# A four-block conv and attention sequence: second attention on f32r tiles with on-chip layout transfers, and jobs ahead of scores in the first attention

## The reference, cut to what matters

```python
# block 0: neighbourhood attention, 8 heads of 16, window 7x7, gate, layer norm
attn = einsum('bijnd,bijnpqd->bijnpq', q, kn) + bias
out = einsum('bijnpq,bijnpqd->bijnd', softmax(attn), vn) @ proj_w + proj_b
x = layernorm(x + out * sigmoid(relu(x @ g1_w + g1_b) @ g2_w + g2_b))
# block 1: depthwise 3x3 convolution without its centre tap, plus x
x = conv(x, kernel * mask) + x
# block 2: full attention, keys and values from the image padded by 3 (reflect)
energy = einsum('bhdq,bhdk->bhqk', q, k)
out = einsum('bhdk,bhqk->bhdq', v, softmax(energy))
x = gamma * out + x
# block 3: Fourier mixing (AFNO), linear attention, MLP of 8*128, three layer norms
```

## Time and profile before

| what | us |
| --- | --- |
| runs | 628.61, 634.68, 642.61 (median 634.68) |
| profiled execution | 639.11, its span 636.9 |
| PE busy | 548.5 (86%) |
| DVE busy | 387.8 (61%) |
| ACT busy | 356.5 (56%) |
| DMA, mean | 36 GB/s |

### The profile page before, as it was taken

How to read it: one execution, slowest core, us unless ns; L and a number is a source line. 1 busy time by engine, 2 the same in 40 slices (tenths; PEclk the granted TensorE clock), 3 DMA queues, 4 the chain that set the end, 5 groups by cost and what they waited for, 6 DMA issues and landing times.

```text
span 636.9 us, 9303 instructions
## 1 busy us (share of the span) xinstructions
PE 548.5 (86%) x3532; PEld 271.1 (43%) x3532; DVE 387.8 (61%) x719; ACT 356.5 (56%) x705; POOL 38.6 (6%) x47
## 2 busy tenths in 40 slices
PE   5889988998989570899999999999998987677997
PEld 2655664555433300122222223222465474553886
DVE  2546654246646390678888888830645645866986
ACT  1777777457432500267777777788764634405553
POOL 5000000011011200200000000000300000000000
PEclk9999999669898755599999999999998998869999
DMA  8500000000005999000160000000000000000000
GB/s 302 245 2 2 1 3 2 0 1 2 1 0 141 121 175 234 2 2 1 30 72 1 1 2 1 3 1 2 0 1 2 1 1 2 1 0 1 0 34 33
DMA packets 8276, 22.65 MB, mean 36 GB/s; under 512 B 1698, under 2 KB 5026, under 8 KB 7074
## 3 DMA queue, kind: packets, MB, share of 16 engines
q1 hardware_dynamic: 8232, 22.06, 14.9%
HBM read 17.80 MB, written 4.19 MB: 35 GB/s over the span
## 4 chain that ended last, share of the span: by engine, by line
PE 69%; ACT 12%; DVE 6%; DMA 6%; SPq 3%; issue 2%; POOL 0%; ACTq 0%
PE ps L392 62%; PE ps L570 6%; DMA scr<-r_o 3%; SPq L445 3%; ACT r_p L1062 2%; DMA r_stk<-mt 2%; ACT r_p L1054 2%; DVE mx L1426 2%; ACT r_p L1026 1%; ACT r_p L1028 1%; ACT r_p L1165 1%; DVE r_p L1500 1%; DVE r_prt L1494 1%; DMA xt<-in_xT 1%; DVE r_prt L1504 1%
## 5 line engine op out<-in xcount | busy, mean ns | idle before, releaser
L392 PE MATMUL ps<-r_stk 98*128 98x512 bf16 (+3 forms) x768 | 164.1, 418 | 29.0 <-DMA r_stk<-mt 16.0
L1165 ACT ACTIVATE r_p<-ps 128x512 f32<-128x512 f32 x256 | 132.5, 624 | 90.8 <-PE ps L392 90.0
L1426 DVE TENSOR_REDUCE mx<-ps 128x1 f32<-128x1024 f32 x128 | 151.0, 1220 | 50.2 <-PE ps L392 50.1
L392 PEld LDWEIGHTS ps<-r_stk 98*128 98x128 bf16 (+2 forms) x768 | 53.7, 131 | 161.1 <-issue 44.6
L392 PE MATMUL ps<-r_p,r_v 128*32 128x512 f32 (+3 forms) x832 | 81.1, 483 | 0.9 <-ACT r_p L1165 0.9
L1351 DVE CUSTOM_DVE_ANT_0 r_p<-ps,r_tab 128x209 f32<-128x209 f32 (+1 forms) x128 | 45.0, 401 | 35.5 <-PE ps L392 35.5
L1054 ACT ACTIVATE r_p<-r_p,mx 128x209 f32<-128x209 f32 (+1 forms) x128 | 57.8, 483 | 3.5 <-DVE mx L1351 3.4
L1062 ACT ACTIVATE r_p<-ps 95x512 f32<-95x512 f32 (+2 forms) x48 | 28.5, 594 | 41.0 <-PE ps L570 41.0
L570 PE MATMUL ps<-cst,r_p 128*95 128x128 f32 (+2 forms) x320 | 47.3, 290 | 2.0 <-ACT r_p L1054 1.1
L570 PEld LDWEIGHTS ps<-cst,r_p 128*95 128x95 f32 (+2 forms) x320 | 38.5, 158 | 21.3 <-ACT r_p L1054 10.5
L1359 DVE COPY r_p<-ps 95x512 f32<-95x512 f32 (+1 forms) x32 | 22.0, 686 | 27.9 <-PE ps L570 27.9
(11 more groups left out here) (185 smaller groups left out, 676.2 us busy)
## 6 DMA issues: line engine op xcount, KB each, us to landing
r_stk<-scr SPq DMA_DIRECT2D x48, 128.0 KB, 8.2
r_tab<-in_tab SPq DMA_DIRECT2D x4, 836.0 KB, 13.3
r_tab<-in_w SPq DMA_DIRECT2D x1, 2688.0 KB, 16.3
scr<-r_prt SPq DMA_DIRECT2D x4, 384.0 KB, 3.0
scr<-r_o SPq DMA_DIRECT2D x4, 384.0 KB, 17.2
cst<-in_cst SPq DMA_DIRECT2D x1, 1124.5 KB, 17.8
r_tab<-in_tab SPq DMA_DIRECT2D x2, 532.0 KB, 7.6
r_tab<-in_tab SPq DMA_DIRECT2D x1, 1064.0 KB, 9.4
```

The costliest lines, as they stand in the source:

```text
L392: return nc.tensor.matmul(out, lhsT, rhs, start=start, stop=stop, **kw)
L1165: nc.scalar.activation(pa2[:, u % 12, :], ps[:, l2_bank(u), :], ACT.Exp).then_inc(sem("exp2"), 1)
L1426: v.tensor_reduce(mx[:, 4 * h + qt:4 * h + qt + 1], ps[:, bank:bank + 2, :], AXIS.XY, ALU.max)\
```

## The change

- **First attention.** On PE `l0_job(s)` stands ahead of `l0_scores(s+1)`. The head outputs are normalised in place.
- **Between.** Only image 0 is prepared ahead of the second attention: convolution, projections with weights whose columns already stand in the order of the stack (`wq2`, `wk2`: each head three times 16 columns in 64), and the values. Stack 0 is made by ACT (the low part, `lw`) and DVE directly in r_stk as f32r.
- **Stacks.** A part is now f32r: high and low, three products of 16 rows, so a head has 48 rows (with the maximum 50) and two heads share a tile at partitions 0 and 64. Stacks 1 to 3 come from `natural2` projections, which ACT moves to xb and POOL splits into nhi and nlo; SP copies them from SBUF to SBUF, 24 DMAs of 64 KB a stack. POOL blanks the stacks' other rows first (`blank`). The buffer scr and its traffic are gone.
- **Maxima.** A first entry is two products, for two heads, into two banks; DVE takes both maxima over 512 keys at once, 16 entries a unit. `maxima` joins the halves and writes the negated maximum as two f32r columns in zmax; `l2_turn` transposes eight blocks of 128x128 on PE, and DVE adds the result to the stack (entry "max"). No DMA.
- **Order.** `l2_order` writes the firsts, maxima and the other jobs (`L2_JOBS`) in one list; `before` spreads a unit's entries over the first 28 of its 32 second products. The denominators, head sums, norm and convolution of image 1, the projections for stacks 1 to 3 and the values of image 1 stand in it. The list has 31 entries up to the first "max", and then 25, 21, 19, 17, 17, 17 and 15 between one "max" and the next.
- **w3.** SP loads it behind the last exponential, since stack 3 lies in r_tab.

```diff
+L2_JOBS = {(0, 0): ("den", 4, 1), (0, 1): ("den", 5, 1), (0, 2): ("den", 6, 1), (0, 3): ("den", 7, 1), (0, 4): ("nproj", 1, 1), (0, 5): ("nproj", 1, 2),
+           (0, 6): ("heads", 0, 1), (0, 8): ("heads", 0, 2), (0, 9): ("gated", 0, 1), (0, 13): ("centre", 0, 1), (0, 14): ("centre", 0, 2),
+           (1, 0): ("centred", 0, 1), (1, 3): ("variance", 0, 2), (1, 6): ("norm", 0, 1), (1, 8): ("conv", 0, 5),
+           (2, 3): ("nproj", 2, 2), (2, 9): ("nproj", 3, 2), (3, 3): ("values", 1, 2)}
...
+    order = []
+    for n in range(2 * NB):
+        for r in range(16):
+            order.append(("first", n, r))
+            if n and r == 1:
+                order.append(("max", n - 1, 0))
+            if (n, r) in L2_JOBS:
+                kind, i, parts = L2_JOBS[n, r]
+                if n == 0:
+                    order.append((kind, i, parts - 1))
+                else:
+                    order += [(kind, i, k) for k in range(parts)]
+    order.append(("max", 2 * NB - 1, 0))
...
+    for n in range(2 * NB):
+        a = at["max", n, 0] + 1
+        b = at["max", n + 1, 0] + 1 if n + 1 < 2 * NB else a
+        before += [a + min((k + 1) * (b - a) // 28, b - a) for k in range(32)]
+    return order, slot, done, at, before
 W3 = [("wq3", C), ("wk3", C), ("wv3", C), ("wo3", C), ("lkg", C), ("lkb", C), ("aw1", 2048), ("aw2", 512),
...
-            sp.wait_ge(sem("pv0"), nblk[NU])
-            sp.wait_ge(sem("og"), NT)
-            sp.wait_ge(sem("lnout"), NT)
-            sp.dma_start(stk[96:98, :, 1].rearrange("p s h n -> p s (h n)"),
-                         io["mrows"].rearrange("p h n -> p (h n)").unsqueeze(1).to_broadcast([2, 3, HG * TOK]))\
-                .then_inc(sem("in_ones"), 16)
-            for t in range(NT):
-                store_parts(2, t)
-                if t % 2:
-                    image_stored(2, t // 2)
-                    load_stack(2, 2 * (t // 2))
-                    if t == 1:
-                        load_stack(2, 1)
+                        rows = slice(64 * a + HD * head, 64 * a + HD * (head + 1))
+                        for r in range(3):
+                            src = (nlo if r == 2 - a else nhi)[rows, :].bitcast(F32)
+                            dst = stack(b)[64 * e + HD * r:64 * e + HD * (r + 1), a, pr, :]
+                            sp.dma_start(dst.bitcast(F32), src).then_inc(sem(f"stk2_{b}"), 16)
+            sp.wait_ge(sem("exp2"), 32 * NB2)
             sp.dma_start(r_tab[:, 0:W3N], io["w3"]).then_inc(sem("in_w3"), 16)
-            for n in range(NB2):
-                b, qh = n // 2, n % 2
-                sp.wait_ge(sem("p1_taken2"), U2 * (n + 1))
-                for h in range(HG):
-                    sp.dma_start(stk[K1_L2:K1_L2 + 2, b % 3, 0, h, tile(qh)], mt[8 * h:8 * h + 8, :]).then_inc(sem("mrow2"), 16)
-                if n == 2:
-                    sp.wait_ge(sem("pv2"), 2 * NCH)
-                    load_stack(2, 3)
             for t in range(NT):
...
+            def project2(j, bank):
+                pr, a = j // 2, 1 - j % 2
+                o = W2A[("wq2", "wk2")[a]][0] + C * pr
+                for t in range(2):
+                    last = mm(ps[:, bank + t, :], w2[:, o:o + C], x2[:, tile(t)])
+                last.then_inc(sem("pj2"), 1)
+
+            def natural2(b, t, bank):
+                o = W2A["wn2"][0] + C * (b % NG)
...
                 if s + 1 < NU:
                     l0_scores(s + 1)
-                l0_job(s)

             pe.wait_ge(sem("tt0"), HG * NU)
...
+            def l2_first(n, r, bank):
+                b, qh, pr, qt, kh = n // 2, n % 2, r // 8, r // 2 % 4, r % 2
+                if r % 8 == 0:
+                    if b:
+                        pe.wait_ge(sem(f"stk2_{b}"), 24 * 16)
+                    else:
+                        pe.wait_ge(sem("sp2"), 2 * pr + 2)
+                q0 = qh * TILE + 128 * qt
+                for e in range(2):
+                    rows = slice(64 * e, 64 * e + PARTS)
+                    last = mm(ps[:, bank + e, :], stack(b)[rows, 0, pr, q0:q0 + 128], stack(b)[rows, 1, pr, tile(kh)])
+                last.then_inc(sem("s1_2"), 1)
+
...
+            def l2_turn(n, bank):
+                pe.wait_ge(sem("zmax"), n + 1)
+                for pr in range(2):
+                    for qt in range(4):
+                        o = C * (4 * pr + qt)
+                        last = nc.tensor.transpose(ps[:, bank + pr, C * qt:C * (qt + 1)], zmax[:, o:o + C], ident)
+                last.then_inc(sem("s1_2"), 1)
+
...
+                pr, rows = h // 2, slice(64 * (h % 2), 64 * (h % 2) + PARTS + 2)
+                mm(ps[:, l2_bank(u), :], stack(b)[rows, 1, pr, 128 * c:128 * c + 128],
+                   stack(b)[rows, 0, pr, tile(qh)]).then_inc(sem("s2_2"), 1)

...
+            issued = 0
+            while issued <= at["max", 0, 0]:
+                l2_entry(issued)
+                issued += 1
+            for u in range(32 * NB2):
+                while issued < before[u]:
+                    l2_entry(issued)
+                    issued += 1
+                l2_second(u)
+                if u % 4 == 3 and u > 4:
...
-                                         ACT.Copy, scale=cc("mult")[:, c:c + 1]).then_inc(sem("vev2"), 1)
+                pr, a, bank = j // 2, 1 - j % 2, (2, 0, 4, 6)[j]
+                act.wait_ge(sem("pj2"), j + 1)
+                if j > 1:
+                    act.wait_ge(sem("sp2"), j - 1)
+                nc.scalar.activation(lw[j % 2], ps[:, bank:bank + 2, :], ACT.Identity,
+                                     bias=vv(("lbq_", "lbk_")[a] + str(pr)), scale=vv(("ls_q", "ls_k")[a])).then_inc(sem("low2"), 1)
...
+            def maxima(n):
+                m = mx[:, 32 * (n % 2):32 * (n % 2) + 32]
+                z, zr = (a.rearrange("p (g x) -> p g x", x=64) for a in (zmax, zmaxr[:, :]))
+                dve.wait_ge(sem("p1"), taken[at["first", n, 15]])
+                v.tensor_tensor(mm16[:, :], m[:, 0:16], m[:, 16:32], ALU.max).then_inc(sem("m16"), 1)
+                dve.wait_ge(sem("m16"), n + 1)
+                if n:
+                    dve.wait_ge(sem("s1_2"), taken[at["max", n - 1, 0]])
+                else:
+                    dve.wait_ge(sem("zero_max"), 1)
+                v.tensor_scalar(zr[:, :, PARTS], mm16[:, :], -1.0, None, ALU.mult).then_inc(sem("zhi"), 1)
+                dve.wait_ge(sem("zhi"), n + 1)
+                v.scalar_tensor_tensor(zr[:, :, PARTS + 1], mm16[:, :], -1.0, z[:, :, PARTS], ALU.mult, ALU.subtract).then_inc(sem("zmax"), 1)
...
+                    o = 32 * (i % 2) + 16 * (k % 2) + 2 * (k // 2)
+                    v.tensor_reduce(mx[:, o:o + 2], ps[:, bank:bank + 2, :], AXIS.X, ALU.max).then_inc(sem("p1"), 1)
+                    if k == 15:
+                        maxima(i)
+                elif kind == "max":
+                    b, qh = i // 2, i % 2
+                    dve.wait_ge(sem("s1_2"), taken[e])
+                    v.tensor_tensor(stack(b)[:, 0, :, tile(qh)], ps[:, bank:bank + 2, :], stack(b)[:, 0, :, tile(qh)].bitcast(F32), ALU.add).then_inc(sem("p1"), 1)
...
+                elif kind == "centred":
+                    dve.wait_ge(sem("cen"), 4)
+                    v.tensor_copy(t1b.rearrange("p (b n) -> p b n", b=2), ps[:, 4:6, :]).then_inc(sem("cenb"), 2)
+                elif kind == "norm":
...
+                pool.wait_ge(sem("vev2"), img + 1)
+                if img == 0:
+                    pool.wait_ge(sem("vsum2"), 4)
+                dims = values2(img)[:, :, :, 0:HD]
+                g.tensor_tensor(dims, dims, cc("mult").unsqueeze(2).unsqueeze(3).to_broadcast([C, NCH, NH, HD]), ALU.mult).then_inc(sem("vsc"), 1)
...
+            def blank(b):
+                for a in range(2):
+                    for i, rows in enumerate((slice(32, 64), slice(96, 128))):
...
+                        g.memset(stack(b)[rows, a, :, :].bitcast(F32), float(a)).then_inc(sem("blank"), 1)
+
+            def natural(b):
+                pool.wait_ge(sem("xb"), b)
+                pool.wait_ge(sem("blank"), 4 if b == 1 else 12)
+                if b > 1:
+                    pool.wait_ge(sem(f"stk2_{b - 1}"), 24 * 16)
+                g.tensor_copy(nhi[:, :], xb).then_inc(sem("nhi"), 1)
+                pool.wait_ge(sem("nhi"), b)
+                g.tensor_tensor(nlo[:, :], xb, nhi[:, :].bitcast(F32), ALU.subtract).then_inc(sem("nlo"), 1)
+
```

More of the change, by code:

```diff
@@ L730, in _, with tap @@
[L730 to L756 removed]
+            def tap(t, k, bank):
+                i = PE_TAPS[k]
+                r0 = 16 * (t % 2) + i // 3
+                return mm(ps[:, bank, :], kd[:, i, :], pad[:, t // 2, r0:r0 + 16, i % 3:i % 3 + W], start=k == 0, stop=k == conv_end)
@@ new lines, in _, with slot_free @@
+            pe.wait_ge(sem("lnout"), 2)
+            for t in range(2):
+                for k in range(len(PE_TAPS)):
+                    last = tap(t, k, t)
+                last.then_inc(sem("conv"), 1)
+            pe.wait_ge(sem("in_w2"), 16)
```

(61 more changed lines are left out.)

474 lines of the change are left out of this document (227 added, 247 removed).

## The result

| | before | after |
|---|---|---|
| median of the runs | 632.9 us (628.6 to 642.6) | 666.4 us (658.6 to 668.3) |
| ratio to before | | 1.051, 95% interval 1.045 to 1.057 |
| profiled execution | 639.1 us | 667.2 us, span 665.3 |

Some executions ran at a lower granted clock and took longer; the ratios leave them out, medians and ranges do not, and the profile of before is of one of them. The changed kernel is 5% slower. The prediction was 608 us, range 591 to 631: it has the wrong sign. The stages of the kernel after, answering to the earlier trace rows: the first attention, the preparation, the first unit of scores, units 0, 1, 4 and 7 of the second attention. Columns: window, its length, busy time of PE, PEld, DVE, ACT and POOL, granted clock, DMA share, GB/s.

What follows compares the result with a forecast made beforehand. PE was taken to set the steady pace before, DVE after; in the first attention, a PE-ACT loop. 15 - 34.8 - 8.4 + 1.2 = -27.0 against the profiled 639.1 gave 612, in the median's terms 608 us, range 591 to 631.

Steps and rivals of the forecast that it cites:

- Part 1: First attention, jobs ahead of scores: scores and later transposes join the loop of PE and ACT, +15 us.
- the upper case: First attention: if its half-clock stretch prices scores at 1.0 us, the reorder costs +20 us.
- Part 2: Preparation of the second attention: splits, stores, loads and their waits go; first reduce at 184.9 instead of 219.7 us, -34.8.
- Part 3: First unit of scores: 28.2 us against 36.7 before, no DMA left in it, -8.4.
- the change of tiling mode: First unit, PE: 16 mode changes round jobs at 0.1 us each, 1.6 us in all.
- Part 4: Eight units of the second attention: 189.4 us against 188.2 before, image 1's work now inside, +1.2.
- DVE is the new bound: Steady unit of the second attention: DVE's work sets 21.4 us, PE needs 20.8 at most; gain 1.95 us a unit.
- Unit 0: Second attention's first unit: 35.5 us with image 1's normalisation and convolution, including 5.5 of DVE waiting, plus 4 for the clock.
- PE stays the bound: Second attention, rival: array halves don't overlap, firsts cost 0.46, units take 24.6 us; +22, 630 us; chance 0.13.
- Stack late: Second attention, rival: stack 1 arrives 10 us late, being fed by three queues in a row; 618 us; chance 0.05.
- Scores cost nothing: First attention, rival: ACT or DVE, not the loop, sets when the next transposes start; 593 us; chance 0.16.
- The clock stays at half in the loop: Second attention, rival: PE's load falls and units run at half clock, 41 us each; three give 666 us; chance 0.07.

Runs made afterwards that it cites:

- E2: Kernel before with only the first attention's job put ahead of the next unit's scores: 660.8 us, ratio to before 1.047.
- E1: Changed kernel with the first attention's scores put back ahead of the job, nothing else: 638.1 us, ratio to before 1.010.
- E4: Changed kernel with scores back ahead of the job and second-attention entries spread evenly over all 32 second products: 618.5 us, ratio to before 0.975.
- E7: E4 with each maximum taken over 2x256 instead of 2x512 columns, work left out, profile only: steady unit 22.77 us.
- E8: E4 with each first product of the first unit issued twice as filler: 633.8 us, ratio to before 1.000.
- E10: E4 with one full f32 filler product ahead of each of the first unit's last eight pairs: 628.6 us, ratio to before 0.997.
- E11: E4 with only the first and last of five parts of image 1's convolution computed, profile only: unit 0 39.2 us, total 616.5 us.
- E9: E5 with the transposes of the maxima moved behind the seventh group's value products: 614.9 us, ratio to before 0.979.
- E5: E4 with pairs of firsts fixed just ahead of a group's second or fourth second product: 620.0 us, ratio to before 0.987.

## Why the prediction was wrong, point by point

**Part 1, +15 predicted; +23.4 in the trace, +25.6 and +28 by E2 and E1.** The mechanism was right, and at full clock the size too, for both kinds of unit: this was no luck. From one iteration's first transposes to the next, the 24 of 31 that ran at full clock in after, E1 and E4 alike sum to +15.9 us. The other seven, which touch a stretch at half clock in after, add 6.1 against E1 and 13.1 against E4, whose first attention happened to keep its clock best. The mis-sized term is half clock: the sum had nothing for it, and 5 us stood in the upper case alone. The mean granted clock of the stage is 0.88 for 0.92 in the earlier trace rows; whether the new order lowers it or the executions differ by chance is open.

**Part 2, -34.8 predicted.** The preparation itself took 21.5 us for the 19.5 of the sum; the convolution ran at half clock at first (10.9 us for 8.75), which is about the whole miss.

**Part 3, 28.2 us predicted, 30.8 measured, for 36.7 before.** The price of the reduce over 2x512 was nearly right (1.22 us for 1.18). One term that failed is the change of tiling mode. In the first unit of after:

```profile
212.48 0.49 PE L435 MATMUL ps<-stkr 48*128 48x512 f32 x2
212.91 1.12 PE L435 MATMUL ps<-r_o,cst 128*128 128x512 f32 x2
213.96 0.49 PE L435 MATMUL ps<-stkr 48*128 48x512 f32 x2
```

A pair and a job of two records take 1.48 us. The pair is 0.23, the job 0.86 by its two passes of 0.43; 0.39 is left for two changes, so 0.2 each and not 0.1: by 16 changes 1.6 us more. The Trainium skill ("TensorEngine Tiling (Array Packing)", Key Properties) says that a change of the tiling mode drains the engine; by that rule I had worked out just this 1.6 and then gone by the row instead. For pairs and jobs the trace agrees with the rule. The row that I had used (bf16 products of 96 and 98 partitions beside f32 value products) was read rightly and did not carry over: there the change into the value products costs 0.09 (0.31 for 0.22 from the last product to them), from f32r products of 50 partitions it costs 0.2 (0.43, where pairs follow each other at 0.23).

The change of mode is not the whole of the 2.6 us. PE took 13.8 us for the first nine pairs and ten job products, not the 12.9 of the sum, and up to there DVE waited 2.6 us for the 2.3 of the sum. Its other 2.6 us are two waits, of 1.36 and 1.21 us, behind jobs at half clock (2.0 us from a job of two records to the next pair, for 1.06); the sum had this unit at full clock.

**Part 4, units: +1.2 predicted, +46.5 measured.** Here the prediction fell, in three steps.

*The steady unit, 21.4 predicted, 25.0 measured.* "DVE is the new bound" was the wrong step; E7 shows it on E4's unit. I added up the work of each engine and took the largest sum. What bounds is a loop with latencies: 1.0 (value products) + 0.53 (second product to exponential) + 0.60 (exponential) + 0.05 + 0.43 = 2.61 us, eight times, and 1.1 for the transposes, so 22.0 us before any wait. In before that loop was hidden, if its latencies were the same there: eight products of 0.23 are 1.84 us against the 1.61 of its part without the value products. Running two products at a time cuts PE's part to 1.2, and the loop gives back only 0.23 of the 0.6 us that this saves. The other 3.0 us of after's unit are the schedule: pairs that open a group (0.23), two groups with three pairs in which PE waits some 0.6 for DVE, and 1.05 of wait at the seam. These waits for DVE follow from the 3.46 us in which it was given nothing, not from its load: with the even spread they shrink to one of 0.7 (E4). I had read the diff's 28 and priced the seam at 0.6 us.

*Unit 0, 39.5 predicted, 50.8 measured, unit 1 24.4 and 34.4.* I had DVE wait 5.5 us for variance and convolution; the wait for the convolution alone was 9.78. It runs with one part ahead of each second product, and DVE's queue holds the reduces behind the sum, so that PE finds no free slot in turn. The clock was 0.73 in unit 0 and 0.54 from 286 to 300 us, where unit 0 ends and unit 1 begins, after PE had waited for DVE. E1, with the same schedule, has 32.2 us for unit 1 at full clock, so some 2 of its 10 us are the clock. With the even spread alone, unit 1 fell from 34.4 to 27.3.

*Unit 6*, 28.7 for 20.9 before: the same schedule, with no jobs, and a mean granted clock of 0.83, which by E8, E10 and E11 may be worth 3 us.

**Rivals.** PE stays the bound because the halves do not overlap (13%): no. A pair costs 0.23, the price of one product, and its members start within 10 ns of each other. The Trainium skill ("TensorE: Matmul & The Clock Gate", Weight-path perf modes) has fast weight load off for FP32; the loads do take 185 ns in place of 99, but they lie beside products. Only behind value products do two starts lie 0.33 apart and not 0.23; whether the 0.1 is a load or the change of mode no run separates. Stack late (5%): no; nothing waited for it, nor for w3. Scores cost nothing (16%): no. The clock stays at half in the loop (7%) had the right time, 666 us, for a wrong reason: units 2 to 5 ran at full clock, and units 0, 1 and 6 in part.

**Forecast signs.** I had written that it is wrong if units stay above 23 us or the first attention does not move from 145. The first shows, 25.0 us. The second does not: the first attention moved, to 168.8 us, further than I had forecast.

Sum of the misses: +8.4 (part 1), +2.0 (preparation), +2.6 (first unit), +45 (units), 58 us; behind the eight units some 3 us came back, so that the profiled execution has 667.2 us where the sum had 612.

## What to carry to other kernels

Adding up each engine's work bounds a stage from below, not more. For every ring of buffers write down the loop through it (producer, latency, consumer, back), and compare it with the sums; an engine made faster only brings the time down to the next loop. Where work is issued from a schedule, look at its seams: a count that stops short of the unit's end starves one engine and then makes the other wait, and it is as cheap to mend as it was to make. An order on one in-order engine (job ahead of scores) must be judged by what the others then wait for: the same instructions in another order cost 26 us.

## What the runs showed of the hardware

- f32r products of 48 or 50 partitions in the two halves of the array do run at once, two firsts or two seconds or one of each: a pair ahead of a group costs 0.23 us (groups of 2.83 and 2.61), as one product does.
- Going between such products and full-array products cost 0.2 us each way, and into value products 0.2 us; from bf16 products of 98 partitions into value products it was 0.09.
- A reduce to two maxima over 2x512 columns takes 1.22 us, that over 2x256 0.69 us.
- With filler products up to 205 us the granted clock was 1.00 and 0.98 up to 210 us (0.75 and 0.67 without them), and then 0.50 for 20 us: here the work that kept it up in one stage did nothing for the next.
- The same code reached the same place up to 11 us apart (first reduce at 176.8 us in E9, 188.2 in E5), with different stretches at half clock.
